# Softmax kept in the scores' PSUM bank, one rounding remainder moved to GpSimd, and scores issued ahead of the attention product

## What is computed

```
x = x + 0.5 * ffn(layernorm(x))
x = x + attention(layernorm(x))
x = x + 0.5 * ffn(layernorm(x))
ffn: 64 experts of rank 16; scores = x Wr^T, softmax over the 16 highest, h = x A, out = (h * gates) B, times 2
attention: 32 heads of 128; q = x wq, k = x wk, v = x wv; causal softmax(q k^T * 192^-0.5) v, then wo
```

## Time and profile before

| | |
|---|---|
| median of 3 runs | 1141.93 us (1141.19 to 1142.91) |
| the profiled execution, its own time | 1145.13 us |
| its span, first to last instruction | 1143.2 us |
| mean granted TensorE clock | 0.988 |
| PE busy | 1092.6 us, 96% of the span |
| DVE, ACT, POOL busy | 709.4, 455.6, 426.2 us |
| chain that ended last | PE 82%, DVE 10%, ACT 4%, issue 3% |

### The profile page before, as it was taken

How to read it: one execution, slowest core, us unless ns; L and a number is a source line. 1 busy time by engine, 2 the same in 40 slices (tenths; PEclk the granted TensorE clock), 3 DMA queues, 4 the chain that set the end, 5 groups by cost and what they waited for, 6 DMA issues and landing times.

```text
span 1143.2 us, 20037 instructions
## 1 busy us (share of the span) xinstructions
PE 1092.6 (96%) x6516; PEld 975.3 (85%) x6516; DVE 709.4 (62%) x1904; ACT 455.6 (40%) x1401; POOL 426.2 (37%) x383
## 2 busy tenths in 40 slices
PE   7999878999999999999999999999999999989998
PEld 7989667889898988888888888888888888978997
DVE  7777655656656575757575657575757575565553
ACT  4112244444444444444444444444444444431111
POOL 5450146343535444344444445353636352010000
PEclk8999999999999999999999999999999999989999
DMA  9400011101010101010201111111011111070000
GB/s 373 193 23 15 1 37 37 56 19 56 18 55 18 55 18 55 18 60 13 73 12 61 32 41 37 37 37 37 37 37 37 37 37 35 2 304 1 28 18 28
DMA packets 13766, 59.67 MB, mean 52 GB/s; under 512 B 1456, under 2 KB 1456, under 8 KB 12720
## 3 DMA queue, kind: packets, MB, share of 16 engines
q1 hardware_dynamic: 13744, 59.38, 14.2%
HBM read 48.63 MB, written 10.75 MB: 52 GB/s over the span
## 4 chain that ended last, share of the span: by engine, by line
PE 82%; DVE 10%; ACT 4%; issue 3%; DMA 1%; POOL 0%; DVEq 0%; SPq 0%; ACTq 0%
PE bank L207 24%; PE bank L209 24%; PE bank L208 24%; DVE prob L719 4%; PE bank L357 3%; PE bank L371 3%; PE bank L347 2%; ACT prob L476 2%; PE bank L248 1%; DVE s7q L741 1%; ACT s7k L431 1%; DVE xa L602 1%; DMA upT_raw<-up_w 1%; PE bank L215 0%; DVE st L594 0%
## 5 line engine op out<-in xcount | busy, mean ns | idle before, releaser
L208 PE MATMUL bank<-wv_hi,xc_lo 128*128 128x256 f32 x512 | 145.2, 284 | 0.0
L209 PE MATMUL bank<-wv_hi,xc_hi 128*128 128x256 f32 x512 | 145.1, 283 | 0.0
L207 PE MATMUL bank<-wv_lo,xc_hi 128*128 128x256 f32 x512 | 145.1, 283 | 0.0
L476 ACT ACTIVATE prob<-prob,nmax 128x128 f32<-128x128 f32 (+1 forms) x256 | 113.5, 445 | 63.3 <-DVE nmax L706 63.3
L853 POOL TENSOR_TENSOR stage_w<-stage_w 128x256 f32<-128x256 f32 x128 | 93.4, 752 | 63.3 <-DMA stage_w<-wqk 60.8
L207 PE MATMUL bank<-xc_lo,wk_hi 128*128 128x512 f32 x224 | 92.4, 412 | 23.2 <-ACT s7k L431 17.9
L719 DVE TENSOR_SCALAR prob<-prob,rinv 128x128 f32<-128x128 f32 (+1 forms) x256 | 108.0, 482 | 0.0
L755 DVE TENSOR_TENSOR x<-bank,x 128x512 f32<-128x512 f32 x128 | 85.2, 685 | 28.1 <-PE bank L209 28.1
L207 PE MATMUL bank<-wo_lo,attT_hi 128*128 128x512 f32 x256 | 100.4, 392 | 0.7 <-DVE attT_lo L589 0.7
L208 PEld LDWEIGHTS bank<-wv_hi,xc_lo 128*128 128x128 f32 x512 | 98.2, 192 | 2.5
L207 PEld LDWEIGHTS bank<-wv_lo,xc_hi 128*128 128x128 f32 x512 | 98.3, 192 | 2.5
(11 more groups left out here) (134 smaller groups left out, 2935.9 us busy)
## 6 DMA issues: line engine op xcount, KB each, us to landing
stage_w<-wqk SPq DMA_DIRECT2D x32, 512.0 KB, 3.3
stage_vo<-wv SPq DMA_DIRECT2D x16, 512.0 KB, 4.5
stage_vo<-wo SPq DMA_DIRECT2D x16, 512.0 KB, 3.2
upT_raw<-up_w SPq DMA_DIRECT2D x4, 544.0 KB, 6.0
keep_up<-upT_hi SPq DMA_DIRECT2D x1, 2176.0 KB, 15.7
keep_up<-upT_lo SPq DMA_DIRECT2D x1, 2176.0 KB, 20.5
upT_hi<-keep_up SPq DMA_DIRECT2D x1, 2176.0 KB, 8.7
upT_lo<-keep_up SPq DMA_DIRECT2D x1, 2176.0 KB, 13.5
```

The costliest lines, as they stand in the source:

```text
L207: nc.tensor.matmul(dst, a_hi, b_lo, start=first, stop=False, skip_group_check=onto)
L208: nc.tensor.matmul(dst, a_lo, b_hi, start=False, stop=False, skip_group_check=onto)
L209: return nc.tensor.matmul(dst, a_hi, b_hi, start=False, stop=last, skip_group_check=onto)
L476: nc.scalar.activation(prob[:, b, a:e], prob[:, b, a:e], ACT.Exp, bias=nmax[:, c:c + 1], scale=-1.0, accum_out=rsum[:, c:c + 1]).then_inc( ...
```

## The change

1. **Softmax in the bank.** The extremum step writes its result back to `sp[b]` instead of `prob`; ACT exponentiates `sp[b]` in place; the normalising multiplication reads `sp[b]` and writes `prob`. ACT waits for both column blocks of a sequence before the first exponential of it.
2. **The lo of C22** (q and k) is computed by GpSimd (`pool_c22`, with semaphores `q22_split`, `k22_split` of its own) instead of DVE. On GpSimd's list the one of q stands between the two parts of the next q weights' split, the one of k behind it.
3. **Scores ahead.** PE issues the scores of unit u+1 behind `fill(1)` of unit u, ahead of unit u's attention product, and waits for both `pT_split` of unit u before them. DVE takes the extrema of u+1 ahead of the split of u's attention product.
4. **In j = 2** ACT takes the snapshot M7 of k ahead of C22's copies of q.
5. **Around the first unit**: the v products of the second half of the first pair move from unit 0 to the stretch ahead of the first scores; there the v product and M2 of k, and on DVE two pairs of steps, change places.
6. **In the prologue** GpSimd splits the first six parts of the first q and k weights in three slices of two parts each.

```
@@ -173
...
             kept upagain_loaded downagain_loaded comb_step comb_hi comb_split
-            wv_hi_s wv_split wo_hi_s wo_split w_sum_s wq_hi_s wk_hi_s wq_split wk_split
+            wv_hi_s wv_split wo_hi_s wo_split w_sum_s wq_hi_s wk_hi_s wpro_hi wq_split wk_split
...
             scores_ready smax_ready exp_done rinv_ready p_ready pT_ready pT_hi_done pT_split
-            q_hi_done q_split k_hi_done k_split
+            q_hi_done q_split q22_split k_hi_done k_split k22_split
@@ -283
         def pe_m1(pe, g, p):
...
             if not isinstance(p, int) or p > 0:
-                pe.wait_ge(s[f"{g}_split"], 4 * p)
+                pe.wait_ge(s[f"{g}_split"], 3 * p)
...
         def pe_m2(pe, g, p):
             if g == "k":
-                pe.wait_ge(s["q_split"], 4 * p + (2 if not isinstance(p, int) or p > 0 else 1))
+                pe.wait_ge(s["q_split"], 3 * p + (2 if not isinstance(p, int) or p > 0 else 1))
             elif not isinstance(p, int) or p > 0:
-                pe.wait_ge(s["k_split"], 4 * p - 2)
+                pe.wait_ge(s["k_split"], 3 * p - 1)
@@ -301
...
             else:
-                pe.wait_ge(s[f"{g}_split"], 4 * p + 1)
+                pe.wait_ge(s[f"{g}_split"], 3 * p + 1)
@@ -340
...
-        def pe_scores(pe, u, j):
-            pe.wait_ge(s["q_split"], u + 1)
-            pe.wait_ge(s["k_split"], u + 1)
+        def pe_scores(pe, p, j):
+            for g in "qk":
+                if j == 2:
+                    pe.wait_ge(s[f"{g}22_split"], p + 1)
+                else:
+                    pe.wait_ge(s[f"{g}_split"], 3 * p + (1, 2, 0, 3)[j])
@@ -376
...
                 used = fill_before(p, j, first)
-                if not (first and j == 0):
-                    pe_scores(pe, u, j)
@@ -394
...
                 def fill(ab):
-                    if j == 0:
+                    if j == 0 and not first:
@@ -422
...
                 fill(1)
+                if j < 3:
+                    pe.wait_ge(s["pT_split"], 2 * u + 2)
+                    pe_scores(pe, p, j + 1)
+                elif not final:
+                    pe.wait_ge(s["pT_split"], 2 * u + 2)
+                    pe_scores(pe, p + 1, 0)
@@ -470
...
         def act_exp(act, u):
             for b in range(2):
+                act.wait_ge(s["smax_ready"], 4 * u + 2 * b + 2)
...
                     c = 2 * b + i
-                    act.wait_ge(s["smax_ready"], 4 * u + c + 1)
-                    nc.scalar.activation(prob[:, b, a:e], prob[:, b, a:e], ACT.Exp,
+                    nc.scalar.activation(sp[b][:, a:e], sp[b][:, a:e], ACT.Exp,
@@ -510
         def act_snap7(act, g, p):
...
             if not isinstance(p, int) or p > 0:
-                act.wait_ge(s[f"{g}_split"], 4 * p - 1)
+                act.wait_ge(s[f"{g}22_split"], p)
@@ -560
...
                     elif j == 2:
+                        act_snap7(act, "k", p + 1)
                         act_c22(act, "q", p + 1)
-                        act_snap7(act, "k", p + 1)
...
                         act_c22(act, "k", p + 1)
-                if j == 0 or (j == 2 and not final):
+                if (j == 0 and not first) or (j == 2 and not final):
@@ -704
...
                     nc.vector.tensor_tensor_reduce(
-                        out=prob[:, b, a:e], in0=sp[b][:, a:e], in1=mask[:, a:e], scale=-SCALE,
+                        out=sp[b][:, a:e], in0=sp[b][:, a:e], in1=mask[:, a:e], scale=-SCALE,
@@ -716
...
                     c = 2 * b + i
-                    nc.vector.tensor_scalar(prob[:, b, a:e], prob[:, b, a:e], rinv[:, c:c + 1], None,
+                    nc.vector.tensor_scalar(prob[:, b, a:e], sp[b][:, a:e], rinv[:, c:c + 1], None,
...
         def dve_low(dve, g, p, i, src):
...
-        def dve_c11(dve, g, p):
+        def dve_c11_sum(dve, g, p):
...
             nc.vector.tensor_tensor(yz[:, :], yz[:, :], s1[:, :], ALU.add).then_inc(s[f"{g}_sum"], 1)
...
+        def dve_c11(dve, g, p):
+            dve_c11_sum(dve, g, p)
@@ -739
...
             nc.vector.tensor_tensor(s7[g][:, :], acc[g][:, :], s7[g][:, :], ALU.add).then_inc(s[f"{g}_sum"], 1)
-            dve_low(dve, g, p, 2, s7[g][:, :])
@@ -783
...
                 if not (first and j == 0):
-                    dve_softmax_max(dve, u)
@@ -811
...
                     dve_normalise(dve, NT, 0, x[:, 0, :])
+                else:
+                    dve_softmax_max(dve, u + 1)
@@ -869
...
                        stage_w[:, a:b, :].rearrange("p i n -> p (i n)"),
-                       s[f"w{g}_hi_s"], 2 * p + part + 1, s[f"w{g}_split"])
+                       s[f"w{g}_hi_s"], 2 * p + part, s[f"w{g}_split"])
...
+        def pool_w_split_sliced(pool, g):
...
+            wait_alone(pool, s["w_sum_s"], 4 * KIND[g] + 3)
+            for n, a in enumerate(range(0, S4, 2)):
+                done = 3 * KIND[g] + n + 1
+                nc.gpsimd.tensor_copy(w_hi[g][:, a:a + 2, :].rearrange("p i n -> p (i n)"),
+                                      stage_w[:, a:a + 2, :].rearrange("p i n -> p (i n)")).then_inc(s["wpro_hi"], 1)
+                pool.wait_ge(s["wpro_hi"], done)
+                last = nc.gpsimd.tensor_tensor(w_lo[g][:, a:a + 2, :].rearrange("p i n -> p (i n)"),
+                                               stage_w[:, a:a + 2, :].rearrange("p i n -> p (i n)"),
+                                               w_hi[g][:, a:a + 2, :].rearrange("p i n -> p (i n)").bitcast(F32),
+                                               ALU.subtract)
+            last.then_inc(s[f"w{g}_split"], 1)
...
+        def pool_c22(pool, g, p):
...
+            pool.wait_ge(s[f"{g}_hi_done"], 4 * p + 3)
+            nc.gpsimd.tensor_tensor(unit_tile(lo_t, g, 2), to_split(s7[g][:, :], g),
+                                    unit_tile(hi, g, 2).bitcast(F32), ALU.subtract).then_inc(s[f"{g}22_split"], 1)
@@ -888
...
             pool_wo(pool, p)
-            if not (final or last_w):
-                pool_w(pool, "q", p + 2)
+            if final:
+                return
+            if not last_w:
+                pool_w_operands(pool, "q", p + 2)
+                pool_w_split(pool, "q", p + 2, 0)
+            pool_c22(pool, "q", p + 1)
+            if not last_w:
+                pool_w_split(pool, "q", p + 2, 1)
+            pool_c22(pool, "k", p + 1)
@@ -992
...
             pool_w_operands(pool, "q", 0)
-            pool_w_split(pool, "q", 0, 0)
+            pool_w_split_sliced(pool, "q")
...
             pool_rstd(pool, 6, 0)
-            pool_w_split(pool, "k", 0, 0)
+            pool_w_split_sliced(pool, "k")
...
                 pool_rstd(pool, t, 1)
-            pool_w(pool, "q", 1)
+            pool_w_operands(pool, "q", 1)
+            pool_w_split(pool, "q", 1, 0)
+            pool_c22(pool, "q", 0)
+            pool_w_split(pool, "q", 1, 1)
+            pool_c22(pool, "k", 0)
@@ -1059
...
             pe_att_transpose(pe, NT - 1)
+            pe_value(pe, 0, 1, 1, wait_bank=False)
             pe_m2(pe, "k", 0)
-            pe_value(pe, 0, 1, 1, wait_bank=False)
+            pe_value(pe, 1, 0, 2)
+            pe.wait_ge(s["xaT_split"], NT)
+            pe_value(pe, 1, 1, 3)
@@ -1144
...
             act_att_transposed_half1(act, NT - 1)
+            act_value(act, 0, 1, 1)
...
             act_c11(act, "k", 0)
-            act_value(act, 0, 1, 1)
+            act_value(act, 1, 0, 2)
+            act_value(act, 1, 1, 3)
@@ -1229
...
             dve_gate_inverse(dve, NT - 1)
+            dve_normalise(dve, NT - 2, 1, x[:, NT - 2, :])
             dve_combined(dve, NT - 3)
-            dve_normalise(dve, NT - 2, 1, x[:, NT - 2, :])
@@ -1239
...
             dve_att_transposed_half1(dve, NT - 1)
+            dve_value(dve, 0, 1, 1)
+            dve_c11_sum(dve, "k", 0)
             dve_combined(dve, NT - 1)
-            dve_c11(dve, "k", 0)
-            dve_value(dve, 0, 1, 1)
+            dve_low(dve, "k", 0, 0, yz[:, :])
+            dve_value(dve, 1, 0, 2)
+            dve_value(dve, 1, 1, 3)
```

## The result

The changed kernel takes **1107.49 us**, the median of 4 runs (1106.99 to 1107.97), beside 1142.42 us for the kernel before on the same chip (1141.19 to 1143.51). The ratio is 0.9694, 95% interval [0.9678, 0.9711]: 3.1% faster. The forecast was 1101.5, range 1097 to 1111. The medians are 34.9 us apart, the spans of the two profiled executions 37.0 (1143.2 and 1106.2), since the profiled execution lies 2.7 us above the median before and 0.5 after. The forecast's sum, made between profiled executions, was 40.4.

A forecast was written before the change was run, and what follows sets the result against it. PE, busy 96%, bounds the kernel and loses 1.83 us per pair through DVE work held by GpSimd. Terms sum to 40.4 us: 1145.1 profiled gives 1104.7, less 3.2 for the median 1101.5; range 1097 to 1111.

The forecast's parts named there:

- pairs: 13 pairs: waits behind DVE work held by GpSimd go, 1.83 us each; 23.4 us gained, lower bound 19.5.
- pair 0, unit 2: Unit 2 of pair 0: the same cure as in later pairs shortens its 17.26 us by 4.4, or 3.1.
- prologue slices: Tile near 80 us: shorter GpSimd instructions let DVE's layernorm output in between; 3.6 us gained, range 2.3 to 4.2.
- layernorm first: Wait before 121.59: layernorm step moved ahead of a 1.21 us subtraction; 2.4 us gained, range 1.1 to 2.8.
- v ahead of the scores: Before the first scores: two v products of 2.88 us each fill idle time; 7.0 us gained, range 5.0 to 7.3.
- M3 of k: Start: its 2.46 us wait shrinks as C22's lo of q goes to GpSimd; 0.7 us gained, range 0 to 1.
- cover gone in pair 0: Units 0 and 1 of pair 0: without the v products, thin margins cost 0.3 us, range 0 to 3.
- last pair: Last pair, without cover: later exponentials and the earlier `pT_split` wait cost 0.8 us, range 0 to 1.5.
- DVE is still held: Rival: multiplications reading `rinv` from SBUF still wait for GpSimd; gains 19.5 and 3.1 instead, 1107 us; chance 0.06.
- 0.1 by my estimate ... nothing is lost: Pairs: later exponentials cost +0.1 us, multiplications from PSUM +0.15; 0.25 fits the 0.7 us slack of unit 1.
- The start gives it back: Rival: GpSimd's k weights or C11 of k come late in pair 0, costing 3 to 7 us; chance 0.15.
- an in-bank chain that outgrows its cover: Rival: slow PSUM to PSUM softmax steps make PE wait in every unit, slower from 0.27 us per step; chance 0.02.

The follow-up runs named there:

- the kernel without the swap: The changed kernel with the snapshot M7 of k put behind C22's copies of q again: 1108.22 us, 0.9697.
- a swap of two products: Kernel with scores behind, extrema ahead; in unit 1 of pair 0, M6 of k before M2, ACT's snapshot M1 before C21's copies: 1100.84 us, 0.9629.

## Why the prediction was right, point by point

The time was inside the range and the mechanism of the pairs stood; the sum was 3.4 us too large. The forecast of the median missed by 6.0, because it also carried over the 3.2 us by which the profiled execution had stood above the median, and now it stands only 0.5 above. Its terms against the two spans:

| term | predicted | measured |
|---|---|---|
| pairs | 23.4 | 21.54 (772.96 - 751.42, 14 periods) |
| pair 0, unit 2 | 4.4 | 4.36 (17.26 - 12.90) |
| prologue slices | 3.6 | 4.16 (17.32 - 13.16) |
| layernorm first | 2.4 | 2.70 (the wait alone 2.37 - 1.23 = 1.14; not undone in a run) |
| v ahead of the scores | 7.0 | 7.34 |
| M3 of k | 0.7 | 1.16 (the wait alone 2.46 - 1.74 = 0.72) |
| cover gone in pair 0 | -0.3 | -2.07 (unit 1 alone -1.84, of which 1.5 the clock) |
| last pair | -0.8 | -1.76 |
| before 80 us, not counted | 0 | -0.46 |
| sum | 40.4 | 36.97 |

- **DVE held by GpSimd** was right: the multiplication with an SBUF operand ends with the GpSimd instruction beside it (1.55 us for one), the same step from the bank takes 0.476 whatever GpSimd does (none of the 256 multiplications, of either form, took more than 0.48), and nothing in the pairs waits. The rival "DVE is still held" is out. The Trainium skill ("GPSIMD Engine Reference", 1. Specifications) says that GpSimd's interfaces to SBUF are shared with DVE, with contention for DVE instructions in a 2-port mode or with two SBUF inputs. The trace agrees for the multiplication and for the subtraction with two SBUF inputs (2.30 us in the earlier trace rows, 0.42 in the earlier trace rows with one input in a bank).
- **The two cures** were priced well one by one, but the prediction let change 1 carry the pairs and named 19.5 us only as a lower bound. The runs showed that change 4 brings nearly this much by itself (53.87: 19.2 us over the 14 periods) and nothing on top of change 1 (53.67 either way).
- **The multiplications in the bank.** The row of L706 gave +0.15 for four; they took 1.38 instead of 0.99, +0.39. The Trainium skill ("VectorE: DVE Perf Modes", the perf-mode tier table and the errata's cycle table) gave 0.66 more, by the prediction's estimate from their formulas. The direction is that of the Trainium skill, the measured size lies between the two. The slack of unit 1 in the pairs bore it: no wait appeared there. What the pairs fell short by does not come from here: with the same multiplications and the scores behind, the period is the 53.53 forecast.
- **"0.1 by my estimate ... nothing is lost"** is the step that failed in the pairs. The scores ahead of the attention product cost 0.14 us per pair without any wait, in PE's own stream: PE is busy the whole 53.67 us, and with the scores behind the period is 53.53. That is 14 x 0.14 = 2.0 us, the whole miss of this term. I had looked for the cost of the order only in waits.
- **Cover gone in pair 0, -0.3.** Of the two margins, that of the k weights held: GpSimd's low part of them ended at 165.56, and PE did not wait for it. Unit 1 waits 0.37 for the probabilities and 1.20 for C21's low part, hardly more than before. The clock fell there where it had not before: 12.38 us instead of 10.54. In the kernel without the swap the same instructions with the same waits ran at a clock of 1.00 and took 10.87, 0.33 more than before, about what the term says. So some 1.5 of the 2.07 is a fall that one execution has and another hasn't. It is bad luck of the profiled one, not a cost shown to belong to the change; without it the sum would be some 38.5. The term put such a fall at nothing in its taken value, since behind the waits of 1.3 in the pairs there was none; its lower bound of -3 held it.
- **Last pair, -0.8.** The mechanism was right. The extrema of unit 62 are ready at 973.4, and the exponentials start at 974.28, behind ACT's copy of an attention product that ends later by the length of the scores. Its 0.35 for the `pT_split` wait was right: that wait is 1.09, now ahead of the scores, where it was 0.72 ahead of the attention product. Too small was 0.15 per unit for the late exponentials. The waits ahead of the transposes grew by 0.16, 0.11 and 0.16 in units 60 to 62 and by 0.38 in unit 63, for which the prediction had nothing, and the transposes themselves take longer: 1.20 us instead of 1.01, 1.00 and 0.82 in units 60, 61 and 63, and 1.55 instead of 1.01 in unit 62. The lower clock is no part of it; it lasts 6.8 us here in both traces.
- **"The start gives it back"**, at 0.15, did not come by either margin it named; the 2.1 us lost in pair 0 are mostly the fall of the clock. The rival of an in-bank chain that outgrows its cover needed 0.27 us more per step. Measured were +46 ns for an extremum and some 40 less for an exponential, so it was never near.

## What to carry to other kernels

Where an instruction on DVE is several times longer than its like, look at what GpSimd does at its end; reading the operand from PSUM, shorter GpSimd instructions, or simply moving another engine's copy ahead of the late one cure the wait behind it, and they overlap, so price each alone and the pair of them. A reordering on the bound engine is to be priced by its own busy period too, not by waits alone. When two kernels are compared by one profile each, look first whether a fall of the clock stands in one and not in the other: here one such fall was worth 1.5 us between two executions of the same instructions, as much as a wait that a swap of two products took away (1.4 us).

## What was not expected of the hardware

- The granted clock after a wait doesn't follow the length of the wait. It fell to 0.86 over unit 1 of pair 0 with waits of 0.37 and 1.20 us, and stayed at 1.00 with 0.72 and 1.20, and over a tile with one of 2.31. Two profiled executions of one kernel show 0.86 in the same window, and an execution of the kernel without the swap, which is the same in every instruction up to there, shows 1.00 with the same waits. What decides it is open.
- ScalarE exponentiates bank to bank in 455 ns (128x256) and 349 (128x128) where SBUF to SBUF took 495 and 395. VectorE's extremum goes the other way, 466 and 313 ns into the bank where it was 420 and 285 into SBUF.
- Scores ahead of the attention product cost PE 0.034 us per unit with no engine waiting. Neither a wait nor the number of switches between kinds of matmul explains it.
